# Scanning both halves of a state in one instruction, with decays in two pairs of PSUM banks and one work bank

## The reference, cut to what matters

```python
xc, z = split(x @ in_w.T)                    # 256 + 256 channels
xc = silu(conv4(xc) + conv_b)                # called u in the kernel
x_dbl = xc @ xp_w.T                          # dt (8), B (16), C (16)
delta = softplus(dt @ dtp_w.T + dtp_b)
A = -exp(A_log)                              # 256 channels x 16 states
h = exp(delta * A) * h + (delta * u) * B_t   # step by step over 256 tokens
y = sum over the 16 states of h * C_t
y = (y + u * D) * silu(z);  out = y @ out_w.T
```

## Time and profile before

| | |
|---|---|
| median of 3 runs | 6018.69 us (6008.41 to 6022.03) |
| profiled execution, span from first to last instruction | 6018.3 us (the page gives no other time for it) |
| DVE busy | 4198.7 us, 70% |
| PE busy | 5016.6 us, 83% |
| POOL busy | 3312.4 us, 55% |
| ACT busy | 3106.3 us, 52% |
| scan stage | from about 97 to about 1896 us of the span |
| one unit of it | 54.76 us |

### The profile page before, as it was taken

How to read it: one execution, slowest core, us unless ns; L and a number is a source line. 1 busy time by engine, 2 the same in 40 slices (tenths; PEclk the granted TensorE clock), 3 DMA queues, 4 the chain that set the end, 5 groups by cost and what they waited for, 6 DMA issues and landing times. The chain is left out here.

```text
span 6018.3 us, 79139 instructions
## 1 busy us (share of the span) xinstructions
PE 5016.6 (83%) x22359; PEld 2504.4 (42%) x22446; DVE 4198.7 (70%) x6070; ACT 3106.3 (52%) x5312; POOL 3312.4 (55%) x2371
## 2 busy tenths in 40 slices
PE   5888888888887888978887999855996899963997
PEld 1333333333332433434343455433664344432664
DVE  5999999999997563056575878643775566652775
ACT  4666666666664454235554777621332577821332
POOL 3888988898885353034443444345343555536333
PEclk8999999999999899989988999966998899976998
DMA  2234322222221002000003333111553443311455
GB/s 79 86 136 152 115 89 89 82 92 89 89 82 39 0 0 85 0 0 0 6 5 79 88 85 93 35 48 66 188 189 107 101 95 97 75 38 51 169 188 175
DMA packets 203028, 494.17 MB, mean 82 GB/s; under 512 B 32432, under 2 KB 57520, under 8 KB 191280
## 3 DMA queue, kind: packets, MB, share of 16 engines
q1 hardware_dynamic: 183536, 451.33, 24.3%
q0 software_dynamic: 18176, 37.79, 1.8%
q10 hardware_dynamic: 960, 0.79, 0.1%
HBM read 381.65 MB, written 108.12 MB: 81 GB/s over the span
## 5 line engine op out<-in xcount | busy, mean ns | idle before, releaser
L396 POOL TENSOR_TENSOR mamba_bu<-mamba_du,mamba_b_all 128x1024 f32<-128x1024 f32 x512 | 1199.4, 2360 | 184.2 <-PE psum L490 168.6
L667 DVE TENSOR_TENSOR_SCAN mamba_bu<-psum,mamba_bu 128x512 f32<-128x512 f32 x1024 | 1190.2, 1207 | 68.9 <-ACT psum L599 34.4
L490 PE MATMUL psum<-mamba_bu,consts 128*128 128x512 f32 x2048 | 965.8, 594 | 8.2 <-issue 5.1
L599 ACT ACTIVATE psum<-mamba_delta,A 128x510 f32<-128x510 f32 x1024 | 682.9, 683 | 386.9 <-DVE mamba_bu L667 373.7
L1646 POOL DMA_INDIRECT results<-ffn_moe_y_rows,ffn_moe_row_of x312 | 303.0, 971 | 507.2 <-DVE ffn_moe_y_rows L1836 426.2
L1761 ACT ACTIVATE ffn_moe_act<-ffn_moe_act 128x512 f32<-128x512 f32 x344 | 217.0, 631 | 688.9 <-DVE ffn_moe_act L1805 484.5
L673 DVE TENSOR_TENSOR mamba_bu<-mamba_bu,psum 128x1024 f32<-128x1024 f32 x448 | 537.3, 1199 | 4.9 <-remote 1.8
L490 PEld LDWEIGHTS psum<-mamba_bu,consts 128*128 128x128 f32 x2048 | 392.7, 192 | 346.1 <-issue 327.8
L2201 POOL TENSOR_TENSOR loc_q_bd<-loc_q_max,weights_l1a 128x512 fp32r<-128x512 f32 x256 | 275.0, 1103 | 379.3 <-DVE loc_q_max L2456 370.7
L2201 POOL TENSOR_TENSOR cau_q_bd<-cau_q_max,weights_l1b 128x512 fp32r<-128x512 f32 x256 | 258.5, 1042 | 243.6 <-DVE cau_q_max L2456 178.1
L2447 DVE TENSOR_REDUCE cau_top<-psum 128x2 f32<-128x512 f32 (+1 forms) x384 | 263.2, 692 | 183.0 <-PE psum L2271 169.2
(11 more groups left out here) (415 smaller groups left out, 11141.9 us busy)
## 6 DMA issues: line engine op xcount, KB each, us to landing
mamba_b_all<-b_rows SPq DMA_DIRECT2D x256, 512.0 KB
ffn_moe_w_gu<-gate_up_parts SPq DMA_DIRECT2D x78, 1024.0 KB
pairs<-empty_rows SPq DMA_DIRECT2D x6, 3432.0 KB, 13.1
ffn_moe_got<-pairs SPq DMA_DIRECT2D x78, 264.0 KB, 3.3
ffn_moe_w_down<-in_l_moe SPq DMA_DIRECT2D x78, 256.0 KB
mamba_c_rows<-b_rows SPq DMA_DIRECT2D x32, 512.0 KB
qk_rows<-loc_qk SPq DMA_DIRECT2D x16, 1024.0 KB, 9.2
ffn_moe_back<-results SPq DMA_DIRECT2D x32, 512.0 KB, 4.7
```

What stands on the lines that cost most here:

```text
L396: nc.gpsimd.tensor_tensor(bu[:, J % BU, :, :], du[:, q % 2, :, :], b, ALU.mult).then_inc(bu_ready, 1)
L490: last = nc.tensor.matmul(ysum[:, h, :], mem.ident, bu[:, J % BU, h, :], start=False, stop=(n == NST - 1), skip_group_check=True)
L599: nc.scalar.activation(by_seq(dA[i % DECAYS])[:, :, 1:S], by_seq(delta[:, q % 2, h, :])[:, :, 1:S], ACT.Exp, scale=mem.A[:, q % 2, h * NST ...
L667: nc.vector.tensor_tensor_scan(bu[:, J % BU, h, :], dA[i % DECAYS], bu[:, J % BU, h, :], 0.0, ALU.mult, ALU.add).then_inc(scanned, 1)
```

## The change

Both halves of a state are scanned by one instruction of 1024 elements. Its decays lie in one of two pairs of neighbouring banks (banks 0 and 1, or 2 and 3); the decays of state J wait until state J - 2 has been scanned, and the scan waits for both halves. The semaphore `scanned` counts states where it counted halves. The c product moves to bank 4. One bank, 5, is left for the front products: each claim waits until the use before has been read. The uses are spread anew: on TensorE dt at states 7 and 9, the output at 10, the gates at 12 and 13; on ScalarE x_dbl at 8, dt at 9 and 11, the output at 13 in front of the last softplus step, both gates at 14 and 15 of the unit before. In `order` the output stands behind the two dt uses.

```diff
--- before.py
+++ after.py
@@ -255,7 +255,7 @@
     CHUNKS = NST // CHUNK
     BU = 8
     LATE = 3
-    DECAYS = 3
+    PAIRS = 2
     POOLED_C = (2, 7)
     b_rows = mem.scratch["b_rows"]
     with ExitStack() as ctx:
@@ -276,8 +276,7 @@
         b_all = sb("b_all", [SLOTS, CHUNK, T])
         c_rows = sb("c_rows", [2, len(POOLED_C), T])
         bu = sb("bu", [BU, 2, T])
-        dA = [mem.bank[i] for i in range(DECAYS)]
-        c_bc, work = mem.bank[3], [mem.bank[4], mem.bank[5]]
+        c_bc, work = mem.bank[4], mem.bank[5]
         ysum = mem.psum[:, 6:8, :]
 
         (xpad_ready, work_ready, work_read, u_ready, z_ready, first_ready, rest_ready, second_ready, parts_ready, c_ready, soft_step, soft_ready, delta_ready, du_ready, bu_ready, dA_ready, scanned,
@@ -292,13 +291,17 @@
 
 
         def front(q):
-            return [("conv", q, 0), ("conv", q, 1), ("xdbl", q, 0), ("out", q - 2, 0), ("dt", q, 0), ("dt", q, 1), ("gate", q, 0), ("gate", q, 1)]
+            return [("conv", q, 0), ("conv", q, 1), ("xdbl", q, 0), ("dt", q, 0), ("dt", q, 1), ("out", q - 2, 0), ("gate", q, 0), ("gate", q, 1)]
 
         order = [use for q in range(UNITS + 2) for use in front(q) if 0 <= use[1] < UNITS]
         position = {use: i for i, use in enumerate(order)}
 
         def by_seq(ap):
             return ap.rearrange("p (b t) -> p b t", b=SEQ_T)
+
+        def decays(J):
+
+            return mem.psum[:, 2 * (J % PAIRS):2 * (J % PAIRS) + 2, :]
 
         def in_time(ap, q):
 
@@ -396,7 +399,7 @@
                 nc.gpsimd.tensor_tensor(bu[:, J % BU, :, :], du[:, q % 2, :, :], b, ALU.mult).then_inc(bu_ready, 1)
 
             def weigh(J):
-                pool.wait_ge(scanned, 2 * J + 2 + LEAD)
+                pool.wait_ge(scanned, J + 1 + LEAD)
                 pool.sem_inc(PASSED[0], 1)
                 q, n = J // NST, J % NST
                 pool.wait_ge(c_landed[q % 2], 16 * (q // 2 + 1) + LEAD)
@@ -428,8 +431,8 @@
         def _(pe):
             def claim(use):
 
-                pe.wait_ge(work_read, position[use] - 1 + LEAD)
-                return work[position[use] % 2]
+                pe.wait_ge(work_read, position[use] + LEAD)
+                return work
 
             def convolve(q, h, half):
                 d = q % 2
@@ -437,7 +440,7 @@
                     if h == 0:
                         pe.wait_ge(xpad_ready, q + 1 + LEAD)
                     claim(("conv", q, h))
-                to = by_seq(work[position["conv", q, h] % 2])
+                to = by_seq(work)
                 for k in (2 * half, 2 * half + 1):
                     last = nc.tensor.matmul(to, mem.conv_in[:, d, k, h * 128:(h + 1) * 128], xpad[:, d, :, k:k + S],
                                             start=(k == 0), stop=(k == 3), skip_group_check=True)
@@ -517,13 +520,12 @@
                             convolve(q + 1, n // 2, n % 2)
                         if n == 5:
                             project_u(q + 1)
-                    if n == 6 and q >= 1:
+                    if more and n in (7, 9):
+                        project_dt(q + 1, int(n > 7))
+                    if n == 10 and q >= 1:
                         out(q - 1)
-                    if more:
-                        if n in (7, 8):
-                            project_dt(q + 1, n - 7)
-                        if n in (11, 12):
-                            project_gate(q + 1, n - 11)
+                    if more and n in (12, 13):
+                        project_gate(q + 1, n - 12)
             for J in range(NST * UNITS - LATE - 1, NST * UNITS):
                 reduce(J)
             out(UNITS - 1)
@@ -593,10 +595,10 @@
             def decay(q, n):
                 if n == 0:
                     act.wait_ge(delta_ready, q + 1 + LEAD)
+                J = NST * q + n
+                act.wait_ge(scanned, J - PAIRS + 1 + LEAD)
                 for h in range(HALVES):
-                    i = 2 * (NST * q + n) + h
-                    act.wait_ge(scanned, i - DECAYS + 1 + LEAD)
-                    nc.scalar.activation(by_seq(dA[i % DECAYS])[:, :, 1:S], by_seq(delta[:, q % 2, h, :])[:, :, 1:S], ACT.Exp,
+                    nc.scalar.activation(by_seq(decays(J)[:, h, :])[:, :, 1:S], by_seq(delta[:, q % 2, h, :])[:, :, 1:S], ACT.Exp,
                                          scale=mem.A[:, q % 2, h * NST + n:h * NST + n + 1]).then_inc(dA_ready, 1)
 
             def out(q):
@@ -624,8 +626,6 @@
                 more = q + 1 < UNITS
                 for n in range(NST):
                     decay(q, n)
-                    if n == 1 and q >= 1:
-                        take_gate(q, 1)
                     if more and n in (3, 5):
                         take_conv(q + 1, int(n > 3))
                     if n == 6:
@@ -633,43 +633,43 @@
                             silu_u(q + 1)
                         silu_z(q)
                         nc.scalar.preload_act_table_set(LN_AND_EXP)
-                    if n == 10 and q >= 1:
-                        out(q - 1)
                     if more:
-                        if n == 9:
+                        if n == 8:
                             take_xdbl(q + 1)
-                        if n in (10, 11):
-                            take_pre(q + 1, n - 10)
+                        if n in (9, 11):
+                            take_pre(q + 1, int(n > 9))
                         if n == 10:
                             round_rest(q + 1)
                         if n == 11:
                             softplus_abs(q + 1)
                         if n == 12:
                             softplus_exp(q + 1)
-                        if n == 13:
+                    if n == 13:
+                        if q >= 1:
+                            out(q - 1)
+                        if more:
                             softplus_ln(q + 1)
-                        if n == 15:
-                            take_gate(q + 1, 0)
-                            if q + 2 < UNITS:
-                                load(q + 2)
+                    if more and n in (14, 15):
+                        take_gate(q + 1, n - 14)
+                    if n == 15 and q + 2 < UNITS:
+                        load(q + 2)
             out(UNITS - 1)
 
         @block.vector
         def _(dve):
-            starts = mem.psum[:, 0:DECAYS, :].rearrange("p a (b t) -> p (a b) t", b=SEQ_T)[:, :, 0:1]
+            starts = mem.psum[:, 0:2 * PAIRS, :].rearrange("p a (b t) -> p (a b) t", b=SEQ_T)[:, :, 0:1]
             nc.vector.memset(starts, 0.0).then_inc(zeroed, 1)
 
             def scan(J):
+                both = bu[:, J % BU, :, :].rearrange("p h t -> p (h t)")
                 dve.wait_ge(bu_ready, J + 1 + LEAD)
-                for h in range(HALVES):
-                    i = 2 * J + h
-                    dve.wait_ge(dA_ready, i + 1 + LEAD)
-                    nc.vector.tensor_tensor_scan(bu[:, J % BU, h, :], dA[i % DECAYS], bu[:, J % BU, h, :], 0.0,
-                                                 ALU.mult, ALU.add).then_inc(scanned, 1)
+                dve.wait_ge(dA_ready, 2 * J + 2 + LEAD)
+                nc.vector.tensor_tensor_scan(both, decays(J).rearrange("p h t -> p (h t)"), both, 0.0,
+                                             ALU.mult, ALU.add).then_inc(scanned, 1)
 
             def weigh(J):
                 dve.wait_ge(c_ready, vector_until[J + 1] + LEAD)
-                dve.wait_ge(scanned, 2 * J + 2 + LEAD)
+                dve.wait_ge(scanned, J + 1 + LEAD)
                 nc.vector.tensor_tensor(bu[:, J % BU, :, :], bu[:, J % BU, :, :], c_bc.unsqueeze(1).to_broadcast([D, 2, T]), ALU.mult).then_inc(weighed_vector, 1)
 
             def gated(q):
```

## The result

The changed kernel takes 6082.68 us (median of 4 runs, 6075.8 to 6084.49) against 6017.77 (4 runs): the medians differ by 65 us. The ratio is 1.010, with a 95% interval of 1.0084 to 1.0117, so it is slower. The forecast was 6058, in a range of 6004 to 6104.

What follows compares the result with a forecast made beforehand. VectorE was taken to pace a unit, with TensorE and ScalarE setting one stretch. From 6018.3 us: -1 for scan, waits and bank, +40 for TensorE's clock falling, +0.4 to the median, giving 6058; range 6004 to 6104.

Steps and rivals of the forecast that it cites:

- forecast 3.2: TensorE before step 9 of every unit: idle 3.2 us in one piece, waiting for weighing 8.
- The first rival: Nothing changes: TensorE's clock holds over the gap, or the loss falls into waits; 6018 us, chance 0.20.
- the clock term: TensorE's clock falls after the gap in each unit, making scan 12 late: 31 x 1.3 = +40 us, bounds 0 to +93.
- Nine units in ten: Share of units in which the clock's fall hits step 9 and delays scan 12; turns 1.45 us into 1.3.
- The price of 1.45 us: Lateness of scan 12 when step 9 loses about 1.6 us to the slow clock, against slack of 0.16.
- The fourth rival: The long slow stretch on TensorE in each unit, 3.0 us a unit: 6110 us, chance 0.07.
- The merged scan: VectorE's scans of states 7 to 15 and the next 0 save 0.06 each: -0.60 us per unit.
- The joint wait: Scan 7 waits for both halves of decay 7, +0.61 us per unit; scan 4's similar wait only just covered.
- What was put at nothing: The single work bank's claims and the moved dt, output and gate uses: each predecessor read in time, no cost per unit.
- a cap on a gain: GpSimd's chain to the next unit's first driven state has 0.6 us to spare, which caps any gain per unit.
- forecast 2: At the start of the stage four handovers become serial: +2 us once.

Runs made afterwards that it cites:

- a1: The changed kernel with three more identity products at state 8, in TensorE's gap behind the claim for the second dt; 1.0003 times the kernel before.
- a2: The changed kernel with the output between the two dts, on TensorE at state 8 instead of 10, on ScalarE at 10 instead of 13; 0.9994 times the kernel before.
- a3: The kernel before with only the output moved, to state 10 on TensorE and 13 on ScalarE; 1.0181 times the kernel before.
- c3: a2 with every half scanned by an instruction of its own, as in a4; 1.000 times the kernel before.
- a4: The changed kernel with each half scanned by its own instruction, waiting for its own half of the decays; 1.0015 times the kernel before.
- b1: The changed kernel with the second dt on TensorE at state 8 instead of 9; 1.0052 times the kernel before.
- b2: a2 with the scan of state 7 alone split into two instructions of 512, each waiting for its own half of the decays; 0.9959 times the kernel before.
- b3: a2 with ScalarE's two silus after decay 7 instead of decay 6; 0.9979 times the kernel before.
- c1: b3 with decay 11 ahead of ScalarE's output and rounding of the rest, and softplus's absolute value after decay 12; 0.9977 times the kernel before.

## Why the prediction was right, and where it was not

**The direction and the cause hold.** TensorE idles 2.86 us in front of state 9 in the full-clock units as in the slow units (forecast 3.2, with dt 0 at 0.86 us; it takes 1.05), the clock falls behind it in half of the units, and dt 1, decay 12 and product 11 pass the delay on. Filling the gap in two ways (a1, a2) brings the clock back, and opening one in the kernel before (a3) brings it down. The first rival (the clock holds) is what a1 and a2 make of the change.

**The two factors of the clock term were both wrong, in opposite ways.** "Nine units in ten" was 15 of 30. The price of 1.45 us was 3.07 and 4.8. I took the stretch for 3.5 us long, losing 1.75; it lasts some 6.8 us in the units of 58.14 and 10.2 in that of 59.85. Only 1.30 of the price is the wait at state 12 that I priced. Product 11, which I gave 0.5 us of slack, is late by 0.75 to 2.34, product 10 by 0.2 to 0.4, and GpSimd by 0.4 more. The fourth rival, 3.0 a unit, was the right price for a slow unit. 31 x 1.3 = 40 stands against 55 measured. That the forecast came within 25 us owes something to luck: half the units at over twice the price gives nearly the same product.

**The merged scan.** It steps by 2.20 us (698.50 to 700.70 in VectorE's timeline after) against 2.19 forecast and 2.25 for the pair: 0.05 saved. The mean durations would give more, 2 x 1.207 before against 2.282 after, 0.13:

```profile
L667 DVE TENSOR_TENSOR_SCAN mamba_bu<-psum,mamba_bu 128x512 f32<-128x512 f32 x1024 | 1190.2, 1207 | 68.9 <-ACT psum L599 34.4
```

But a scan's last 0.08 us overlap the next instruction (2.28 long, 2.20 to the next start), and this part a merge does not save. The page "VectorE: DVE Perf Modes" of the Trainium skill, in its section on the fixed extra latency of SBUF-source operations, would have had 0.157; the step between scans shows a third of that, and here the measurement decides. c3 says the same in a run.

**The joint wait.** +0.61 forecast, and from gating to scan 7 it is 9.62 us where it was 9.01: +0.61. Scan 4 waits 0.80, and gating comes on time, as argued: covered, and only just.

**What was put at nothing and was not.** A full-clock unit was to be 0.06 us shorter and is 0.31 longer. Of these 0.37, 0.27 is VectorE's new wait for GpSimd at state 0, and about 0.1 is that ten scans save 0.05 each in place of 0.06. The output at state 10 stands in front of reduction 7, on which GpSimd waits for a ring slot before it drives state 15, and that chain had 0.6 us to spare. In the kernel before GpSimd does not wait there; now it does:

```profile
458.78 2.36 POOL L399 TENSOR_TENSOR mamba_bu<-mamba_du,mamba_b_all 128x1024 f32<-128x1024 f32 x1 [1.02 <-PE psum L493]
```

I had named the chain and its spare time as a cap on a gain, and did not ask what the moved output does to it. a2, with the output in front of another reduction, has the wait no more. The start of the stage cost 3.9 us up to the first scan (36.53 after the memset, 32.66 before), forecast 2; unit 0 gives 2.5 of it back. In that unit the two slow stretches of before do not occur, nor does VectorE's wait of 1.80 us.

## What to carry to other kernels

A product that is moved leaves a hole where it stood: look first for what the moved work was hiding, and at TensorE's longest unbroken idle time, not its busy share. When engines feed one another within tenths of a microsecond, follow each chain through the moved instruction, those of the engines that are not the bound too. Merging instructions that already overlap saves little, and a joint wait can cost more; a split at the one place where the wait falls keeps both.

## What the runs showed of the hardware that was not expected

The number of slow units does not go by the length of the gap alone. Gap and slow units of 30: 2.93 us in a3, 30; 2.86 in the changed kernel, 15 and, on another chip, 13; 2.39 in a4, 5; 1.81 in b1, 12. None is slow in the kernels whose gap at this place is closed (a1, a2, b2, b3, c1, c3), nor in the kernel before between its first gating and its last unit. Single gaps say the same. In unit 0 of the changed kernel one of 3.08 us leaves the clock up, since the four passes behind it take 1.88 us:

```profile
166.07 1.88 PE L493 MATMUL psum<-mamba_bu,consts 128*128 128x512 f32 x4 [3.08 <-DVE mamba_bu L673]
```

And a gap of 2.07 us late in the units of 58.14 brings no fall, where one of 2.06 to 2.09 us at the same place brings one in every slow unit of b1.

Nor is it chance from unit to unit, for the order is regular. In the changed kernel groups of 2, 3, 2, 5 and 3 slow units stand between groups of 2 or 3 at full clock, and the last unit of each such group is its only one of 59.84 us or more. On the other chip the groups are of 2 or 3 units and once of one, and end in the same way, but for unit 30, which is slow by itself. In b1 every second or third unit is slow. So it looks as if the time at which a gap falls counts, and that shifts with the length of the units before it; this is a reading of the pattern and no run tests it. The units' own length differs between these kernels as well, and none of the runs varies one without the other.

A slow stretch can also be followed by another. Work at half clock is late, GpSimd with it, and VectorE's longer wait for GpSimd makes a later gap of TensorE longer. In one unit of the changed kernel (60.13 us) that wait is 0.96 us in place of 0.27 and that gap 2.35 us in place of 1.65; the clock falls again, and scan 4 waits 1.99 us. In b1 a second fall comes in every slow unit.
